# First attention of a four-block kernel: query-key prologue of a batch moved one period ahead of its scores, and split into its own square root

## The reference

```python
h = _ln(x, ln1_g, ln1_b)
q, k, v = jnp.split(h @ w_qkv + b_qkv, 3, axis=-1)      # 16 heads of 8
kc = jnp.concatenate([previous bucket of k, k], axis=2) # buckets of 64
scores = jnp.einsum('bnihd,bnjhd->bnhij', qb, kc) * scale
scores = jnp.where(mask, scores, -jnp.inf)
attn = jax.nn.softmax(scores, axis=-1)
ob = jnp.einsum('bnhij,bnjhd->bnihd', attn, vc).reshape(B, T, C)
x = x + ob @ w_out + b_out
h2 = _ln(x, ln2_g, ln2_b)      # then the gelu network
```

## Time and profile before

| what | value |
| --- | --- |
| median of 3 runs | 1055.04 us |
| the profiled execution | 1056.1 us |
| its span | 1054.3 us |
| first attention within the span | 0 to about 273.8 us |
| PE busy over the span | 917.5 us (87%) |
| DVE | 822.5 us (78%) |
| ACT | 748.9 us (71%) |
| POOL | 431.6 us (41%) |
| mean granted TensorE clock | 0.951 |
| kq reads, issue to landing, median | 2.9 us |
| heads writes, issue to landing, median | 2.2 us (high), 2.0 us (low) |

### The profile page before, as it was taken

One profiled execution on the slowest core, in us unless ns is written; L12 is line 12 of the kernel. 1 busy time (PEld: TensorE's weight loads), 2 busy tenths in 40 slices (PEclk: granted clock), 3 DMA queues, 4 the chain that ended last, 5 costly groups with the idle time before them and its releaser, 6 DMA issues. The chain is left out here.

```text
span 1054.3 us, 28529 instructions
## 1 busy us (share of the span) xinstructions
PE 917.5 (87%) x9966; PEld 576.0 (55%) x9966; DVE 822.5 (78%) x2280; ACT 748.9 (71%) x1482; POOL 431.6 (41%) x613
## 2 busy tenths in 40 slices
PE   3688888887799999999999999869888865899995
PEld 2466656665355444444444444446556544788862
DVE  4587787875477799868899989958888867888854
ACT  1256666666799888888888878547677644688854
POOL 4255666667245200000000011014588877676653
PEclk9598999999799999999999999979999985999999
DMA  6635555541100000032122222111111102233318
GB/s 192 211 116 173 174 185 165 164 139 33 32 1 1 2 1 1 1 95 80 67 73 80 83 60 79 32 34 51 32 46 51 58 27 76 73 86 85 83 48 217
DMA packets 85578, 84.50 MB, mean 80 GB/s; under 512 B 8978, under 2 KB 62484, under 8 KB 85440
## 3 DMA queue, kind: packets, MB, share of 16 engines
q1 hardware_dynamic: 76240, 71.49, 22.0%
q0 software_dynamic: 4544, 8.60, 2.5%
q10 hardware_dynamic: 4656, 2.59, 0.9%
HBM read 45.77 MB, written 37.78 MB: 79 GB/s over the span
## 5 line engine op out<-in xcount | busy, mean ns | idle before, releaser
L931 ACT ACTIVATE d__hf<-keep__banks,dense__d 128x512 f32<-128x512 f32 x288 | 185.5, 680 | 48.2 <-PE keep__banks L1169 47.2
L995 DVE TENSOR_TENSOR d__hl<-d__hf,d__hh 128x1024 f16<-128x1024 f32 x144 | 174.1, 1220 | 28.0 <-ACT d__hh L936 25.8
L936 ACT ACTIVATE d__hh<-d__hf 128x1024 f16<-128x1024 f32 x144 | 152.2, 1057 | 4.6
L915 POOL TENSOR_SCALAR d__rstd<-d__mv 128x4 f32<-128x4 f32 x16 | 13.9, 869 | 336.7 <-DVE d__mv L1123 336.7
L411 POOL TENSOR_SCALAR_AFFINE_SELECT a__pt<-a__pt 128x512 f32<-128x512 f32 x128 | 81.5, 660 | 93.6 <-ACT a__pt L446 93.6
L1167 PE MATMUL keep__banks<-dense__xh,dense__w1h 128*128 128x512 f16 x288 | 109.9, 382 | 2.9 <-ACT d__hf L931 1.7
L1167 PE MATMUL keep__banks<-d__hh,dense__w2h 128*128 128x512 f16 x288 | 109.2, 379 | 2.4 <-DVE d__tmp L1052 2.4
L1169 PE MATMUL keep__banks<-dense__xh,dense__w1l 128*128 128x512 f16 x288 | 109.9, 381 | 0.0
L1168 PE MATMUL keep__banks<-dense__xl,dense__w1h 128*128 128x512 f16 x288 | 109.9, 381 | 0.0
L1168 PE MATMUL keep__banks<-d__hl,dense__w2h 128*128 128x512 f16 x288 | 109.2, 379 | 0.0
L1169 PE MATMUL keep__banks<-d__hh,dense__w2l 128*128 128x512 f16 x288 | 109.2, 379 | 0.0
(11 more groups left out here) (353 smaller groups left out, 2330.8 us busy)
## 6 DMA issues: line engine op xcount, KB each, us to landing
rows<-a__blank SPq DMA_DIRECT2D x72, 268.0 KB, 3.8
d__G<-gates SPq DMA_DIRECT2D x64, 256.0 KB, 3.1
a__kq<-heads SPq DMA_DIRECT2D x48, 128.0 KB, 2.9
c__xin<-rows SPq DMA_DIRECT2D x39, 134.0 KB, 2.3
heads<-a__high SPq DMA_DIRECT2D x32, 128.0 KB, 2.2
dense__stage<-e_w SPq DMA_DIRECT2D x16, 256.0 KB, 3.6
b__stage<-e_w SPq DMA_DIRECT2D x32, 128.0 KB, 2.3
heads<-a__low SPq DMA_DIRECT2D x16, 128.0 KB, 2.0
```

What stands on the lines that cost most here:

```text
L931: act.activation(hf[:, q, f], HB[:, f], gelu, scale=1.0 / WS, bias=b1[:, at:at + 1]).then_inc(s_["h_free"], 1)
L936: act.activation(hh[:, j % (LEAD + 1), f - 1:f + 1], hf[:, q, f - 1:f + 1], ACT.Copy).then_inc(s_["hi_done"], 1)
L995: dve.tensor_tensor(hl[:, p, f], hf[:, q, f], hh[:, p, f], ALU.subtract).then_inc(s_["lo%d_done" % i], 1)
```

## The change

The table is written anew. `norm`, `lift`, `qk` and `low` of a batch now stand in parts 3 and 4 of the period of its statistics (period n), so two periods before its scores instead of one. `norm2` moves from the end of a period to the front of the next. The root is split: `xpower` (`power` on POOL, columns 0:2, semaphores `var_done`, `rstd_done`) and `power2` (columns 2:4, `var2_done`, `rstd2_done`). SP issues the 0.5 MB of x rows and the other large loads later by one batch: behind the `kq` reads of batch 0 and of batch 1. Nothing is computed otherwise than before.

```diff
 PARTS_0 = [
-    [("scores", 2, 0), ("lift", 1, 0), ("vproj", 2, 0), ("shift", 3, 1), ("qk", 1, 0), ("xstats", 0, 0), ("low", 1, 0),
-     ("weights", 3, 0), ("values", 4, 3), ("copy", 4, 1)],
+    [("scores", 2, 0), ("norm2", 6, 0), ("vproj", 2, 0), ("shift", 3, 1), ("xstats", 0, 0),
+     ("weights", 3, 0), ("xpower", 0, 0), ("values", 4, 3), ("copy", 4, 1)],
     [("scores", 2, 1), ("mpad", 2, 0), ("output", 5, 0), ("back", 4, 1),
      ("weights", 3, 1), ("values", 3, 0), ("halves2", 6, 0), ("wlow", 0, 0)],
-    [("scores", 2, 2), ("shift", 2, 0), ("stats", 0, 0),
+    [("norm", 0, 0), ("scores", 2, 2), ("lift", 0, 0), ("shift", 2, 0), ("stats", 0, 0),
      ("weights", 3, 2), ("power", 0, 0), ("values", 3, 1), ("copy", 3, 0)],
-    [("scores", 2, 3), ("mpad", 2, 1), ("back", 3, 0), ("norm", 0, 0),
-     ("weights", 3, 3), ("values", 3, 2), ("norm2", 5, 0), ("split", 0, 0)]]
+    [("scores", 2, 3), ("mpad", 2, 1), ("qk", 0, 0), ("back", 3, 0), ("low", 0, 0), ("sums", 0, 0),
+     ("weights", 3, 3), ("values", 3, 2), ("split", 0, 0)]]
...
             sp.wait_ge(loaded, 16 * LOADS)
-            sp.dma_start(x[:, 4:12, :], d["x"][:, 4:12, :]).then_inc(x_mid, 16)
-            sp.dma_start(keep["gate0"][:], d["gate0"]).then_inc(gate_in, 16)
...
                 if n == 0:
+                    sp.dma_start(x[:, 4:12, :], d["x"][:, 4:12, :]).then_inc(x_mid, 16)
+                    continue
+                if n == 1:
                     sp.dma_start(x[:, 12:NT, :], d["x"][:, 12:NT, :]).then_inc(x_rest, 16)
                     keep["fetch_dense"](sp)
+                    sp.dma_start(keep["gate0"][:], d["gate0"]).then_inc(gate_in, 16)
                     sp.wait_ge(blank_set, 1)
...
-                for i in range(5 * n, min(5 * n + 5, BLANKS * NC_)):
+                for i in range(5 * n - 5, min(5 * n, BLANKS * NC_)):
...
             def power(n):
                 pool.wait_ge(var_done, n + 1)
-
-                wait(pool, norm2_done, n - 5)
...
-                t, v = Tally(pool, pool_ln, 1, n), both_norms(n)
...
+            def power2(n):
+                pool.wait_ge(var2_done, n + 1)
+
+                wait(pool, norm2_done, n)
...
-                if what == "power" and n:
+                if what == "xpower" and n:
                     power(n)
-                if what == "norm" and n >= 5:
+                if what == "power" and n >= 5:
+                    power2(n - 5)
+                if what == "sums" and n >= 5:
```

More of the change, by code:

```diff
@@ L193, in parts_0 @@
                 if what == "lift":
-                    if s > 0:
-                        step(what, s - 1, k)
-                elif what in ("xstats", "stats", "power", "norm"):
+                    if s < NB + 4:
+                        step(what, s, k)
+                elif what in ("stats", "power", "sums"):
                     if s < AHEAD + 5:
@@ L267, in attention_0 @@
         var_done = m.sem("var_done")
-        rstd_done = m.sem("rstd_done")
-        pool_ln = m.sem("pool_ln")
+        var2_done = m.sem("var2_done")
+        rstd_done, rstd2_done = m.sem("rstd_done"), m.sem("rstd2_done")
+        pool_ln, pool_ln2 = m.sem("pool_ln"), m.sem("pool_ln2")
         passed_pool, passed_dve = m.sem("passed_pool"), m.sem("passed_dve")
@@ L300, in cut_of @@
             return keep[names[a]][:, e * CT:(e + 1) * CT]
-        def both_norms(n):
-            return slice(0 if n < NB else 2, 4 if n >= 5 else 2)
         def toks2(n):
@@ L364, in power @@
                 pool.wait_ge(var_done, n + 1)
-                wait(pool, norm2_done, n - 5)
                 settle(pool, passed_pool)
-                t, v = Tally(pool, pool_ln, 1, n), both_norms(n)
-                t.link(pool.tensor_scalar(rstd[:, v], mv[:, v, 1], EPS, 1.0, ALU.add, ALU.mult))
-                pool.tensor_tensor(rstd[:, v], rstd[:, v], half[:, v], ALU.pow).then_inc(rstd_done, 1)
+                t = Tally(pool, pool_ln, 1, n)
+                t.link(pool.tensor_scalar(rstd[:, 0:2], mv[:, 0:2, 1], EPS, 1.0, ALU.add, ALU.mult))
+                pool.tensor_tensor(rstd[:, 0:2], rstd[:, 0:2], half[:, 0:2], ALU.pow).then_inc(rstd_done, 1)
+            def power2(n):
+                pool.wait_ge(var2_done, n + 1)
+                wait(pool, norm2_done, n)
+                settle(pool, passed_pool)
+                t = Tally(pool, pool_ln2, 1, n)
+                t.link(pool.tensor_scalar(rstd[:, 2:4], mv[:, 2:4, 1], EPS, 1.0, ALU.add, ALU.mult))
+                pool.tensor_tensor(rstd[:, 2:4], rstd[:, 2:4], half[:, 2:4], ALU.pow).then_inc(rstd2_done, 1)
             pool.memset(half[:], -0.5).then_inc(half_set, 1)
@@ L384, in step @@
             def step(what, n, k):
-                if what == "power" and n:
+                if what == "xpower" and n:
                     power(n)
-                if what == "norm" and n >= 5:
-                    pool.wait_ge(rstd_done, n + 1)
+                if what == "power" and n >= 5:
+                    power2(n - 5)
+                if what == "sums" and n >= 5:
+                    pool.wait_ge(rstd2_done, n - 4)
                     pool.tensor_scalar(shift2[:], mv[:, 2:4, 0], -1.0, 1.0, ALU.mult, ALU.mult).then_inc(shift2_own, 1)
@@ L399, in step @@
                                        cut_of(("w1h", "w2h"), n), ALU.subtract).then_inc(w_low, 1)
-                if what == "norm" and n < NB:
+                if what == "sums" and n < NB:
                     rows_landed(pool, n)
@@ L486, in _ @@
                 dve.memset(t[:, 0:BK], 0.0).then_inc(cleared, 1)
-            for t in kq[0:2]:
-                dve.memset(t[:], 0.0).then_inc(kq_clear, 1)
+            dve.memset(kq[0][:], 0.0).then_inc(kq_clear, 1)
+            dve.memset(kq[1][:], 0.0).then_inc(kq_clear, 1)
             sums = Tally(dve, ln, 0, 0)
@@ L500, in step @@
                     dve.wait_ge(cleared, CLEARS)
-                if what == "xstats" and n < NB:
+                if what == "xstats":
                     wait(dve, rstd_done, n)
@@ L509, in step @@
                         ins = dve.bn_aggr(mv[:, a, :], st[:, a, :])
-                        ins.then_inc(var_done, 1) if a and n < 5 else sums.inc(ins)
+                        ins.then_inc(var_done, 1) if a else sums.inc(ins)
                 if what == "stats" and n >= 5:
-                    wait(dve, rstd_done, n)
                     wait(dve, shift2_done, n - 5)
@@ L519, in step @@
                         ins = dve.bn_aggr(mv[:, 2 + a, :], st[:, 2 + a, :])
-                        ins.then_inc(var_done, 1) if a else sums.inc(ins)
-                if what == "norm" and n < NB:
+                        ins.then_inc(var2_done, 1) if a else sums.inc(ins)
+                if what == "norm":
                     wait(dve, lift_full, n)
```

## The result

The changed kernel takes 1047.63 us, the median of 7 runs (1043.98 to 1050.35), beside 1055.03 for 7 runs of the kernel before (1052.45 to 1057.11): a ratio of 0.9934 with a 95% interval of 0.9909 to 0.996. It is faster by 0.7%, and not by the 2.4% that was forecast; 1047.63 lies above the range of 1020 to 1042.

The account below looks back on a forecast made before the run. A loop of waits over several engines was taken as the bound. A 13.2 us period saves 18.5 in the middle, the start 6.3: 1056.1 becomes 1031.3, or 1030 as median; range 1020 to 1042 us.

Parts of the forecast that it names:

- the loop: First attention: waits over several engines set the 14.57 us period; ACT's `norm2` and `split` delay the copy before the projection.
- the own root: POOL issues two root pairs instead of one: under 1 us more POOL work, priced at zero.
- the start: Up to batch 3: 7.34 us wait gone, 1.0 lost twice, 1.0 gained in later periods; net 6.3 us less.
- the port: DVE's `norm` runs beside POOL instructions and slows through the shared port: 0.67 us per period, bounds 0 and 1.8.
- my loop sum of 12.54: Longest loop per period, through the normalisation: PE 4.91, scores to maximum 0.86, DVE 6.77 us.
- part 2 of the sum: What bounds after the change: a 12.54 us loop through the normalisation, PE waiting about 1 us at `lift`, DVE nearly full.
- my rival on the clock: PE's stops at `lift` drop its clock to 1.2 GHz: 4.8 us more per period, 1064 us at 7 periods; chance 0.05.
- The two cases that gave 1044 and 1045: Rivals for the middle: whole-instruction port lock, 1044 us, chance 0.08; another loop near the old period, 1045 us, chance 0.09.
- the whole-instruction price of the port: Each `norm` operation waits out a whole POOL instruction: 1.8 us, period 14.34, time 1044 us; chance 0.08.
- another loop through ACT: A loop through ACT and POOL holds the period at 14.45 us, middle gain 3.4, time 1045 us; chance 0.09.

Follow-up runs that it names:

- the two experiments that took about half of it or more away: Changed kernel with eight filler turns and `norm` ahead of `output` and `back`, 1032.67 us; with four and POOL's two remainders ahead of the next period's mask 0, 1029.4 us.
- the filler: Changed kernel plus useless identity turns on PE before its wait for `hn` at `lift`: four turns 1029.16 us, twelve turns 1031.48 us.
- both moves: Changed kernel with `norm` placed behind `mpad`, ahead of `output` and `back`, and `lift` placed after values 1: 1042.12 us, ratio 0.9904.
- one move: Changed kernel with only `lift` placed after values 1, 1034.4 us, or only `norm` placed behind `mpad`, ahead of `output` and `back`, 1034.48 us.
- twenty turns for batch 1: Changed kernel with twenty useless identity turns before batch 1's `lift` and four before the others: 1035.8 us, ratio 0.9817.

## Why the prediction was wrong

**Right: the loop.** The copy behind `norm2` and `split` was part of the bound, and with the new table the period comes free of it. No run takes back the own root or the new place of `norm2` alone, so how much each part of the change gave is not shown. The two shortest periods are 12.77 us with DVE at 12.00, and with the clock kept the stretch from batch 3 to batch 15 takes 157.35 us against the forecast 156.4. The order in which things come next was right too: PE waits for `hn`, ACT no longer waits ahead of the projection, `kq` is in time.

**Right in the number: the start.** 5.4 us against 6.3; batch 0 at 19.34 (19.2 forecast), batch 1 at 30.41 (31). In part this is luck. I put nearly the whole gain on the order of the loads, 7.34 us less the small losses. With the old order in the new table 3.3 of the 5.4 us are there all the same (62.42 for 65.68 at batch 3), and the order gives 2.2; alone it gives 1.2. That it gains next to nothing without the new table I had not seen.

**Nearly right: the port.** 0.85 us against 0.67. I put it on the loop, and the two experiments that took about half of it or more away gained 0.1 us a period and no time. I also called the pair of rows beside the mask at 51.69 the only one; the trace of before has a second, 0.66 and 0.70 us from 66.74. The 12.77 us of a period in which it is fully paid show that my loop sum of 12.54 plus 0.67 was somewhat too long there.

**The step that failed** is in part 2 of the sum: "PE then waits about 1 us at each `lift`; that is the next late thing". I priced that wait at nothing since DVE would be the bound. It is 1.8 us in most periods, one piece (with the port in it; my rival on the clock had 1 to 1.6), in a stage where PE had been working almost without a stop. With most of these waits the clock falls to 1.2 GHz for some three to seven microseconds, and that was priced at nothing. PE then becomes the bound for that part of the period. From batch 3 to batch 15 this costs 171.09 less 157.35, **13.7 us**, or 1.2 us in each of 11 periods. Another 2.0 lie before batch 3 (60.25 for 58.22). Execution against execution the miss is 16.3 us (1047.6 for 1031.3): 14.7 in the middle (171.09 for 156.4), 13.7 of which the filler gives back; 0.9 at the start; 2.3 in what follows the dense block's start, where nothing was changed; less the 1.5 gained behind batch 15.

**I had the mechanism as a rival, with the wrong price and the wrong weight.** I gave the clock 0.05, on one counterexample: a period of before in which PE waited 0.97 us at the turn and 0.84 at the projection with PEclk at 1.00. A total of 1.8 in two pieces kept the clock in each period of before that has them. But that trace has also a single wait of 1.71 us at the turn that kept it, in a period of 12.92 us (timeline of PE; busy time by stretch):

```profile
68.15 0.41 PE L602 MATMUL keep__banks<-keep__ident,a__hn 128*128 128x128 f32 x2 [1.71 <-DVE a__hn L527]
```

```profile
68.15:81.07 12.92, 11.23 (x300) 8.65 (x301) 11.18 (x33) 7.33 (x16) 6.98 (x13) 1.00 0.35 99
```

And the stretch at the low level that I quoted, 95 to 100 us, begins between 93 and 94 us, as a wait of PE of 1.03 us ends (93.78). So waits of one size do both, and neither one period nor one rule of length could settle the chance. What the runs show is how often: in the changed kernel eight of the ten waits at the turn of 1.33 us or more come with a hit, and with four turns of filler one period in 11 is hit. I also priced a period hit at 4.8 us, as if PE ran all of it at the low level, so the rival came out as a loss (1064 at 7 periods). A period hit has a PEclk of 0.88 or 0.79, not 0.50, and lies 1 to 1.6 us (13.84 to 14.38) or 2.9 (15.7) over 12.77. The mean price is less, 1.2 us in each period, because with the clock kept some periods are longer than 12.77 too (13.61 and 13.64 beside 12.70, with four turns of filler). Eight of 11 periods are hit and the kernel is still faster. The place for this case was between the forecast and the old time, and I had no case there for it. The two cases that gave 1044 and 1045 did so for other reasons: the whole-instruction price of the port, which the 12.77 us rule out, and another loop through ACT, which the filler rules out.

## What to carry to other kernels

A wait that costs nothing on a path can still cost the clock. When a change gives PE a longer single wait in each period, price that wait by the clock as well, and by the part of the period that runs low, not by all of it. The test is cheap: a few useless matmuls in front of the wait, and the same ones in the kernel before as a control. A transfer moved behind another only pays if the engine that waits for it has nothing urgent queued behind that wait.

## What the runs showed of the hardware

- In the changed kernel the granted clock of PE went to its low level with single waits of 1.75 to 2.57 us, before their end or up to two microseconds behind it, with DVE and POOL busy meanwhile, and stayed there for up to almost seven microseconds of unbroken work (PEclk 0.50 from 154 to 160 us, 0.65 in the next). Hits of both sizes follow waits of the same 1.80 us (15.73 us from 184.10, 14.27 from 169.83), the long and the short taking turns. Waits of 1.02, 1.33 and 1.57 us kept it at 0.98 to 1.00. Of the equal waits of 1.70 us in the kernel with both moves, the one at 80.56 kept it and the one at 93.84 did not (0.38 and 0.59 us for the same four matmuls). In other kernels the two cases overlap: 1.71 us in the kernel before kept it, and 1.09 us with `lift` behind values 1 kept it twice and lost it twice (1.08 lost it too). So the length of a single wait does not decide it. What else the clock answers to stays open. The Trainium skill (TensorE: Matmul & The Clock Gate, "A second HAM failure mode: psum-queue depth-cycling") tells of a kernel in which TensorE pauses so often and so briefly between groups of matmuls that the clock swings between its two levels. This case's traces agree as far as the swing goes, which follows waits of 0.8 to 2.6 us; here there are one or two of them in a period.
- Turns of the identity, four in 0.60 us, were enough to keep it in all but one period: PEclk 0.99 for 0.87 over the stretch from 60 to 215 us.
- PEclk over that stretch, beside the time: 0.87 for 1047.6, 0.88 for 1042.1 (both moves), 0.93 for 1034.4 and 0.94 for 1034.5 (one move), 0.99 for 1029.2 and 1.00 for 1031.5 (filler). It parts these versions of the new table into three groups and does no more. With the old load order it is 0.89 for 1049.1. With twenty turns for batch 1 it is 0.99 for 1035.8, so the clock does not account for that time. The kernel with POOL's remainders behind `power` has 0.97 and takes 1046.5, since its loss is a wait for the mask.
- Open: why with the clock kept some periods take 13.6 us and others 12.7 (two of the long ones with four turns, 13.64 and 13.72, hold a PE wait of 0.7 to 0.8 us for nothing that the profile shows); whether the last 0.4 us of the port would count if both `norm` rows were short and no mask late, and why the first two periods run partly at the low clock. No run settled these.
